# A four-layer block with a two-way scan on one core: GpSimd operations twice as wide, a ring of four scan states, attention scores issued two heads at a time, shared weight buffers and a new table of slots

## What is computed

```
x = x + L0_attn(layernorm(x))   # 16 heads of 16; scores (q k)^2, causal, divided by their sum; then Wo
x = x + L0_ffn(layernorm(x))    # int8 weights, 256 -> 768 -> 256, silu(gate) * up
x = x + L1_attn(layernorm(x))   # two scans, forward and over the flipped sequence:
                                #   u, z = split(x Win); u = silu(conv4(u)); dt = softplus(...)
                                #   h = exp(dt A) h + (dt u) B;  y = sum over 16 states of h C
                                #   y = (y + u D) silu(z);  out = y Wout
x = x + L1_ffn(layernorm(x))    # blockwise fp4 quantise of x, of the weights and of the hidden
                                # values, 256 -> 704 -> 256
```

## Time and profile before

| | us |
|---|---|
| median of 3 runs | 6741.94 |
| lowest and highest | 6723.36, 6750.02 |
| the profiled execution, its own time | 6731.3 |
| its span, first to last instruction | 6729.6 |

### The profile page before, as it was taken

One profiled execution on the slowest core, in us unless ns is written; L12 is line 12 of the kernel. 1 busy time (PEld: TensorE's weight loads), 2 busy tenths in 40 slices (PEclk: granted clock), 3 DMA queues, 4 the chain that ended last, 5 costly groups with the idle time before them and its releaser, 6 DMA issues.

```text
span 6729.6 us, 82733 instructions
## 1 busy us (share of the span) xinstructions
PE 5027.9 (75%) x21900; PEld 3136.3 (47%) x21900; DVE 4791.3 (71%) x6116; ACT 4129.1 (61%) x6696; POOL 4928.8 (73%) x3914
## 2 busy tenths in 40 slices
PE   3787777778778777877768777777877777787666
PEld 2344444454445444454444545444444544545444
DVE  3157777676877778687676867767687776868774
ACT  1366666666666666666666666666666666666563
POOL 0077777777777877778777777878777777777785
PEclk6678888888888888888888888888888888888777
DMA  3011111111111111111111111111111111111110
GB/s 111 15 43 38 51 45 47 38 47 45 50 51 47 45 42 45 46 51 50 40 50 40 50 45 48 45 38 53 40 50 51 47 47 38 45 46 48 37 46 26
DMA packets 152792, 308.76 MB, mean 46 GB/s; under 512 B 20870, under 2 KB 58310, under 8 KB 149926
## 3 DMA queue, kind: packets, MB, share of 16 engines
q1 hardware_dynamic: 152278, 302.80, 14.4%
HBM read 285.90 MB, written 16.84 MB: 45 GB/s over the span
## 4 chain that ended last, share of the span: by engine, by line
PE 47%; DVE 17%; issue 13%; POOL 11%; ACT 10%; DMA 1%; DVEq 0%; SPq 0%; POOLq 0%; ACTq 0%
PE psum L1497 8%; PE psum L1307 8%; POOL arena_m L723 5%; DVE arena_m L1214 4%; PE psum L1351 4%; PE psum L1422 3%; PE psum L1477 3%; PE psum L1430 3%; DVE arena_m L1164 3%; POOL arena_m L734 3%; PE psum L1385 3%; PE psum L1367 2%; PE psum L1439 2%; DVE arena_m L1225 2%; PE psum L1413 2%
## 5 line engine op out<-in xcount | busy, mean ns | idle before, releaser
L723 POOL TENSOR_TENSOR arena_m<-bS,arena_m 128x512 f32<-128x512 f32 x2048 | 2621.8, 1297 | 305.6 <-PE psum L1497 231.3
L1214 DVE TENSOR_TENSOR_SCAN arena_m<-psum,arena_m 128x512 f32<-128x512 f32 x2048 | 2448.0, 1209 | 322.4 <-POOL arena_m L723 193.6
L1497 PE MATMUL psum<-ident,arena_m 128*128 128x128 f32 x8192 | 1437.2, 312 | 540.1 <-DVE arena_m L1225 289.2
L734 POOL TENSOR_TENSOR arena_m<-arena_m,hc 128x512 f32<-128x512 f32 x1024 | 1307.3, 1277 | 569.0 <-ACT hc L951 345.7
L943 ACT ACTIVATE psum<-arena_m,Aneg 128x512 f32<-128x512 f32 x2048 | 1396.1, 690 | 428.2 <-DVE arena_m L1214 382.9
L1497 PEld LDWEIGHTS psum<-ident,arena_m 128*128 128x128 f32 x8192 | 1103.8, 160 | 1180.5 <-issue 535.6
L1225 DVE SCALAR_TENSOR_TENSOR arena_m<-psum,Ct,arena_m 128x512 f32<-128x512 f32 x1024 | 747.3, 730 | 379.8 <-PE psum L1497 375.0
L1307 PE MATMUL psum<-arena_a 64*128 64x512 f32 (+3 forms) x2048 | 829.2, 528 | 205.3 <-ACT arena_a L815 79.4
L951 ACT ACTIVATE hc<-psum,Ct 128x512 f32<-128x512 f32 x1024 | 696.3, 680 | 375.3 <-PE psum L1497 300.7
L815 ACT ACTIVATE arena_a<-psum 128x384 f32<-128x384 f32 (+1 forms) x768 | 401.8, 525 | 452.9 <-PE psum L1307 425.5
L1307 PEld LDWEIGHTS psum<-arena_a 64*128 64x128 f32 x2048 | 369.6, 208 | 541.3 <-issue 231.9
(11 more groups left out here) (151 smaller groups left out, 7216.9 us busy)
## 6 DMA issues: line engine op xcount, KB each, us to landing
bS<-brow SPq DMA_DIRECT2D x512, 256.0 KB, 3.2
wB<-kept_B SPq DMA_DIRECT2D x16, 1408.0 KB, 6.2
wU<-kept_U SPq DMA_DIRECT2D x32, 512.0 KB, 4.5
wZ<-kept_Z SPq DMA_DIRECT2D x32, 512.0 KB, 4.6
wO<-kept_O SPq DMA_DIRECT2D x32, 512.0 KB, 4.8
wA<-kept_A SPq DMA_DIRECT2D x16, 768.0 KB, 5.6
wB<-kept_B SPq DMA_DIRECT2D x16, 768.0 KB, 4.3
wA<-kept_A SPq DMA_DIRECT2D x16, 640.0 KB, 4.2
```

The lines of the kernel that those rows point to most:

```text
L723: pool.tensor_tensor(hb[s % HBS][:, m, :], bS[:, s % 2, :], du[r][:, m, :], ALU.mult).then_inc(m_dbu.sem, 1)
L734: pool.tensor_tensor(yT[:, 2 + i, :], yT[:, 2 + i, :], hc[:, i, :], ALU.add).then_inc(m_yl.sem, 1)
L1214: dve.tensor_tensor_scan(v, EB[j % EBS], v, 0.0, ALU.mult, ALU.add).then_inc(m_scan.sem, 1)
L1497: ins = pe.transpose(HT[pos % 2][:, m * P:(m + 1) * P], hb[s % HBS][:, m, i * P:(i + 1) * P], ident[:, :])
```

## The change

1. **GpSimd works on 128x1024.** `inflow` forms two channel groups with one operation, every other slot, four slots ahead instead of three. `add_last` adds both token groups of a state with one operation, and `hc` has two pairs of buffers.
2. **Four states in the ring** (`HBS = 4`), and the turning of a state comes six slots behind the scan instead of four (`TURN = 6`); add and weigh follow at seven, eight and nine. Token groups 0 and 1 now go to VectorE and 2 and 3 to ScalarE, in that order.
3. **Scores of two heads at once.** `score` does nothing in even steps and in odd ones issues the products of two heads, alternating between partitions 0 to 63 and 64 to 127, into two PSUM banks. `weigh` does a whole group of four heads at a time; its bank is kept only from its slot until the division. Squares are written by key group, so that the unit of key groups 2 and 3 takes two operations of ScalarE for one. The mask is four operations of 128x512 for a group, before two of 128x512 and one of 128x1024.
4. **Softplus** rewritten: ScalarE has one more operation (Identity, for 1 + exp), VectorE one less.
5. **Shared weight buffers.** `wZ` is `wU`, `wX` lies in `wO`. So four loads now wait for the other user of the buffer: z's weights for the end of the products with u's, and so on.
6. **fp4 weights behind attention.** The setup turns and stores only the other weights. No engine waits for the stores before its first slot of block -2. In block -1, SyncE stores them at slot 0 and loads the fp4 weights, VectorE quantises in slots 12 to 17, TensorE turns from slot 36 on, SyncE stores at slot 56; all wait for the stores at slot 92.
7. **All rows of the table have other slots.**

```diff
-    HBS = 3
+    HBS = 4
-    ORDER = (0, 2, 1, 3)
+    TURN = 6
...
-        wZ = sb("wZ", [P, KD, DI])
-        wX = sb("wX", [P, NM, P])
+        wZ = wU
         wO = sb("wO", [P, NM, D])
+        wX = wO[:, 0:NM // 2, :].rearrange("p m (h c) -> p (m h) c", h=D // P)
...
-        row("a_weigh", None, 1, PE=[17.1, 19, 22, 26, 27, 31.1, 35, 37, 40.1, 44, 46, 48])
+        row("a_weigh", None, 1, PE=[19, 29, 39, 49])
...
-        HELD = range(14, 53)
+        divided = [j for j in range(SLOTS) for q in PLAN["DVE"][j] if q[0] == "a_sums"]
+        held = {}
...
-                pool.tensor_tensor(hb[s % HBS][:, m, :], bS[:, s % 2, :], du[r][:, m, :], ALU.mult).then_inc(m_dbu.sem, 1)
+                two = slice(m, m + 2)
+                pool.tensor_tensor(hb[s % HBS][:, two, :], bS[:, s % 2, :].unsqueeze(1).to_broadcast([P, 2, T]), du[r][:, two, :],
+                                   ALU.mult).then_inc(m_dbu.sem, 1)
...
-                pool.tensor_tensor(yT[:, 2 + i, :], yT[:, 2 + i, :], hc[:, i, :], ALU.add).then_inc(m_yl.sem, 1)
+                pool.tensor_tensor(yT[:, 2:4, :], yT[:, 2:4, :], hc[:, s % 2, :, :], ALU.add).then_inc(m_yl.sem, 1)
...
-                act.activation(lx[:, c, :], src, ACT.Ln, bias=1.0).then_inc(m_ln.sem, 1)
+                act.activation(src, cx[:, c, :], ACT.Identity, bias=1.0).then_inc(m_w.sem, 1)
+                act.wait_ge(*m_w.by(b, q + 1))
+                act.activation(lx[:, c, :], src, ACT.Ln).then_inc(m_ln.sem, 1)
...
-                dve.tensor_scalar(cx[:, c, :], src, 1.0, -1.0, ALU.add, ALU.add).then_inc(m_c1.sem, 1)
...
+                    if first(b) and FP4_DVE <= j < FP4_DVE + 6:
+                        fp4_weights(j - FP4_DVE)
...
+                if w % 2 == 0:
+                    apart(pe)
+                    return
                 for i, c in UNITS[un]:
                     n = T - i * P
-                    ins = pe.matmul(bank("a_score", None, w)[:, c:c + n], kT[rows, ht, i * P:(i + 1) * P], qm[rows, j, i * P:T],
-                                    start=True, stop=True)
+                    for half in range(2):
+                        rows = slice(64 * half, 64 * half + 64)
+                        ins = pe.matmul(bank("a_score", None, w - 1 + half)[:, c:c + n], kT[rows, ht, i * P:(i + 1) * P],
+                                        qm[rows, j, i * P:T], start=True, stop=True)
```

518 lines of the change are left out of this document (280 added, 238 removed).

## The result

| | before | after |
|---|---|---|
| median us (lowest to highest) | 6743.27 (6723.36 to 6750.02) | 6626.63 (6622.97 to 6628.53) |
| the profiled execution, its own time | 6731.3 | 6625.01 |
| its span | 6729.6 | 6623.3 |
| first scan, last scan, behind it | 367.8, 6619.8, 109.8 | 281.1, 6507.4, 115.9 |

The ratio is 0.983, with a 95% interval of 0.981 to 0.9852: 117 us faster, where 283 were forecast. The last line of the table says where they went. The setup gave 86.7 us, more than the 75 forecast. From the first scan to the last it is 6252.0 before and 6226.3 after, 1.6 us a block instead of 13. That is from one profiled execution of each kernel, and single runs of the kernel before lie 27 us apart, 1.7 us a block; so the blocks' gain is hardly told from none. The nine blocks in the middle take 397.9 us before and 396.3 after, in the mean.

A forecast was written before the change was run, and what follows sets the result against it. Four engines bind in turn, TensorE most often (under 47% of the chain). Terms of -13 us a block, -208 over 16 blocks, plus setup -75 gave 6448 profiled, 6459 us predicted (-4.2%), range 6170 to 6710.

The forecast's parts named there:

- Setup, -75: Before the first scan: fp4 work moved behind attention saves 75 us once, bounds -50 and -100.
- The rival on it: The fp4 work is not hidden: 47 us come back, 6506 us, first scan after 320; chance 0.07.
- Scores, -15: TensorE in attention: paired score products overlap, halving their busy time; -15 us a block, from 0 to -25.
- GpSimd -4: GpSimd's inflow and addition: 1024-column operations take 22 us a block off it, worth -4, from 0 to -18.
- VectorE behind it +8: VectorE's small norm operations wait longer behind GpSimd's wider ones: +8 us a block, from 0 to +17.
- ScalarE, +2: ScalarE's extra squares and Identity operations cost +2 us a block, from 0 to +10.
- Ring, banks, loads and rows, -4: Ring, PSUM banks and shared-buffer loads priced at nothing, new table slots at -4 us a block, from +10 to -20.
- Both covers of "three slots": SyncE's waits for z's second half (slot 46) and X's weights (slot 78) each have three slots, 9 us, to spare.
- The slack wins: Rival: four states and free banks let gains come together, -32 us a block, 6155 us; chance 0.22.
- The pairs don't overlap: Rival: paired scores on TensorE gain nothing, +2 us a block, 6699 us; chance 0.13.
- GpSimd holds VectorE: Rival: VectorE, held by GpSimd, ends every stretch; +17 us a block, 6939 us; chance 0.08.

The follow-up runs named there:

- alternate halves: Kernel before, with scores of neighbouring steps reading partitions 0 to 63 and 64 to 127 in turn, heads mixed up: 6609.44 us, ratio 0.982.
- the version put together: Changed kernel with ScalarE weighing one slot behind the turning, GpSimd operations of 512 columns and three SyncE entries behind row loads: 6394.56 us, ratio 0.9508.
- the moved entries: Changed kernel with SyncE table entries moved behind loads of rows of B: four moved 6677.67 us; three, x's load left in slot 87, 6617.44 us.
- the old softplus: Changed kernel with ScalarE's Identity taken away and VectorE's second operation put back: 6636.17 us, ratio 0.9861.
- the short lag: Changed kernel with ScalarE weighing a turned token group one slot behind the turning instead of two: 6480.58 us, ratio 0.9641.

## Why the prediction was right and wrong

**Sign and range** held (6627 in 6170 to 6710), and the time lies 168 us above the forecast.

**Setup, -75: the sum right, because two larger terms cancelled.** The first layer norm starts at 35.21 where 40 was said, and the fp4 quantising runs from 62.5 to 110.5, where I had 60 to 107. The first scan comes at 281.1 for 293. The first division is VectorE's L1134, the scores are TensorE's L1377; the last two lines are from TensorE's own timeline.

```profile
35.21 1.40 DVE L1095 BATCH_NORM_STATS2 stats<-xA 128x6 f32<-128x256 f32 x4
...
62.54 1.22 DVE L1043 TENSOR_REDUCE hc<-arena_m 88x64 f32<-88x1024 f32 x1 [5.85 <-DMA arena_m<-in_L_ffn_w_down]
...
110.43 0.25 DVE L1134 RECIPROCAL rz<-psum 128x16 f32<-128x16 f32 x1
```

```profile
82.74 0.92 PE L1377 MATMUL psum<-arena_a 64*128 64x384 f32 x4 [0.43 <-ACT arena_a L859]
111.45 1.65 PE L1377 MATMUL psum<-arena_a 64*128 64x256 f32 x8 [27.79 <-issue]
```

The first division does stand right behind the quantising, as feared, and more hangs on it than was said. Scores of the next groups do not go on: the next one needs the PSUM bank that the division gives back (`take_bank`), so TensorE stands still for 27.8 us, from 83.7 to 111.45, and ScalarE with it. I had at most 17 us, from a division due at 90; it was due at 82. The pairs paid for it: they are worth 28 us in this stretch (the run with both products in the same rows), and from the first norm to the first scan it is 245.9 us, 250.6 before. So 27.8 of the 47 us of fp4 work are not hidden. The rival on it falls by its own sign, a first scan after 320, but only because the pairs' gain was there to meet it; that the two are equal is luck.

**Scores, -15: the mechanism right, the size too large.** The busy time fell by 44% (829 to 467 us), near the half that was said. In the old table the overlap gave 5.9 us a block (alternate halves), the pairing 2.9 more in the new one; 8.8, between the bounds of 0 and -25. I had taken the scores' share of the chain as what would come back, and that share did not come back whole. Taken away from the changed kernel, the overlap costs 24 us a block, part of it through the clock, so what an overlap is worth depends on how close the table packs the scores. The Trainium skill's "TensorE: Matmul & The Clock Gate", Part 3, led me to an estimate of 35% saved for a pair; the runs measure 46% of what the same products cover in one half (863 to 467 us), part of it through the clock.

**GpSimd -4 and VectorE behind it +8, together +4: near, for reasons that were half wrong.** The wide operations take 2.37 us as said. Undoing them gives 1.1 us a block in the changed kernel, not to be told from none, and 4 in the version put together, where it is clear. So there the width costs, as the net of both terms said; for the change itself it isn't shown. But the small operations' sum fell in the change, from 326 to 281 us, where I expected an average above 1.2 us; it is 0.70. One operation is held longer, as foretold, but fewer are held (167 of 400 take over 0.3 us, 284 before). In slots 88 to 96 that is because they run in a wait of GpSimd's, as the moved entries showed; for the others it is likely. I had priced the hold by the length of GpSimd's operations; the moved entries show that it counts as much whether GpSimd pauses at that place. The Trainium skill's "GPSIMD Engine Reference", section 8, names the contention, for VectorE's operations with two SBUF inputs or in a 2-port mode. The step held longest here (L1102) has one input, and no view shows its mode. That a hold can last 11.6 us over ten operations no row that I had taken out showed; the trace of before has one of 6.5 us over six, which I had not looked for.

**ScalarE, +2: sign not settled, size small.** I had called it the least full engine beside a stretch where VectorE is less full (65.5 for 69.0 of 105 us); in the other three stretches it holds. The third square cost nothing: 768 squares were busy for 401.8 us before, 1024 are for 380.3. ScalarE's busy time rose by 81 us, Identity's, and the old softplus gives no gain.

**Ring, banks, loads and rows, -4: the step that failed, beside the size of the scores' term.** I counted the fourth state and the longer lag as slack for GpSimd's addition and did not set the slot in which ScalarE reads a bank beside the slot in which TensorE needs it again. That cost 9.2 us a block (8.0 by the ratios), and the term, with what the account below leaves over, came out at +6 instead of -4: inside its bounds, on the bad side, as the scores were on theirs. Both covers of "three slots" were tested by the change itself: behind z's weights (slot 46) there is no wait, behind X's (slot 78) there is one of 4.5 us, and in the changed kernel it cost nothing. The longest wait, behind the store of rows in slot 26, I had not listed at all.

**The account of a block:** overlap -5.9, pairing -2.9, the late bank +9.2, the width +1.1 make +1.5, and -1.6 was measured. The remaining -3 hold the new table of slots with its longer stretch from slot 46 to 92, the ring and the softplus, and the error of single executions, about 1 us a term, and the error of adding parts that were measured in different surroundings: overlap and lag both have prices that differ by a factor of four to five between the two tables. So the sum is an order of size and no proof that nothing else moved.

**The rivals.** "The slack wins" (6155) was kept off in part by the bank that came late; with the short lag, narrow operations and three entries moved the time is 6382 to 6395, half of the way from the changed kernel to there. The ground that I gave against it, four engines above 73%, was misread: ScalarE is at 66 and 67% in that part. "The pairs don't overlap" is out. "GpSimd holds VectorE" was right as a mechanism and wrong in its place. A wait that takes the place of the one removed was the right class of rival, and I had looked for it on the wrong engine.

## What to carry to other kernels

When a double-buffered PSUM bank changes its reader or its lag, write down for each use the slot of the last read and the slot of the next write, and count the slots between: at zero, the writer runs in step with the reader and all that the reader waits for. Work that is moved behind another layer is hidden only if nothing behind it on its engine gives back a bank. A wait on an engine that isn't the bottleneck may be the gap in which a neighbour's small operations run; before removing it, look at what stands beside it. And an overlap of products is worth what the next engine leaves of it, so measure it where it will stand.

## What the runs showed of the hardware

- Products of 64 rows in different halves of the array's rows overlap even when each is issued behind a wait of its own: 2048 of them cover 593 us where the same products in one half cover 863 (at a lower clock), and 467 in pairs behind one wait.
- With the scores in one half the mean granted clock in their stretch was 0.70 of full speed, with pairs 0.87.
- With ScalarE's weighing a slot later in the old kernel, the mean granted clock of the whole kernel was 0.78 for 0.83, and the same TensorE work was busy for 390 us more.
- A VectorE operation of 128x4 can be held not only until GpSimd's current operation ends but over a run of ten of them, 11.6 to 12.2 us, in 10 of 16 blocks of one execution. With operations of 512 columns it came also once at 12.1 us (short lag and narrow), six times at 7.2 (only the width undone) and once at 6.5 (the kernel before); with 1024 columns once, 9.9 us, in the run with the short lag and four entries moved.
- Splitting a ScalarE operation of 384 columns into one of 256 and one of 128 cost no busy time: 768 squares cover 402 us, 1024 over the same columns 380. Neighbours in the list overlap at their ends: the lengths of the 1024 add up to 451 us.
